# Attention products of a cross-attention + FP4 FFN kernel: operands as fp16 halves with one power of two per batch, and a new instruction order in the loop body

## What is computed

```python
# x, ctx: (32, 256, 512) f32
def xattn(q, k, v):                       # q = layernorm(x), k = v = ctx
    t, p, g = Wt @ v, Wp @ q, Wg @ k      # per batch, Wt/Wp/Wg: 256 x 256
    att = einsum('bgcd,bgcd->bg', p, g) * 0.125      # 8 groups of 32 channels
    y = Wz_g @ (att * t)                  # per group, 32 x 32
    return groupnorm(y) * gamma + beta + v
x = x + xattn(layernorm(x), ctx, ctx)
def ffn(x):                               # D = 512, H = 1408
    gate, up = q4(x) @ q4(w_gate).T, q4(x) @ q4(w_up).T
    return q4(silu(gate) * up) @ q4(w_down).T        # q4: blockwise FP4 rounding, 16 values a block
x = x + ffn(layernorm(x))
```

## Time and profile before

| | |
|---|---|
| median of 3 runs | 1738.39 us (1738.07 to 1740.09) |
| the profiled execution, own time | 1737.87 us |
| its span | 1736.0 us |
| PE busy | 1680.2 us (97%) |
| DVE busy | 1506.6 us (87%) |
| ACT busy | 825.9 us (48%) |
| POOL busy | 722.1 us (42%) |
| granted PE clock | 0.998 |

### The profile page before, as it was taken

The page is one execution under the profiler, slowest core; times in us unless marked ns, Lnnn a source line. Parts: engine busy times, 40 slices in busy tenths (PEclk is TensorE's granted clock), DMA queues, the critical chain, the costliest instruction groups (busy, mean ns, idle before and its releaser), DMA issues.

```text
span 1736.0 us, 27880 instructions
## 1 busy us (share of the span) xinstructions
PE 1680.2 (97%) x8723; PEld 919.5 (53%) x8723; DVE 1506.6 (87%) x2577; ACT 825.9 (48%) x1472; POOL 722.1 (42%) x951
## 2 busy tenths in 40 slices
PE   2799999999999999999999999999999999999999
PEld 1665555555555555555555555555555555555544
DVE  7877888889888888988898898889888988888887
ACT  3665454544445444444545444454444444545322
...
DMA packets 412150, 155.86 MB, mean 90 GB/s; under 512 B 383200, under 2 KB 384480, under 8 KB 412128
## 3 DMA queue, kind: packets, MB, share of 16 engines
...
...
## 4 chain that ended last, share of the span: by engine, by line
PE 91%; POOL 6%; DVE 1%; DMA 1%; issue 1%; ACT 0%; SPq 0%; POOLq 0%; DVEq 0%; ACTq 0%
PE pairs L550 52%; PE work L561 25%; PE work L500 5%; PE work L512 3%; PE work L527 2%; PE ubank L527 2%; POOL raw L1863 2%; POOL raw L1852 1%; POOL w_parts L1863 1%; POOL w_parts L1852 1%; DMA raw<-in_L_ffn_w_gate 0%; DMA hT_parts<-raw 0%; POOL xc L1786 0%; PE pairs L580 0%; POOL q_parts L1802 0%
## 5 line engine op out<-in xcount | busy, mean ns | idle before, releaser
L550 PE MATMUL pairs<-w_gate_hi,xT_parts 128*128 128x512 f16 (+1 forms) x1536 | 555.4, 362 | 1.5 <-DMA xT_parts<-raw 1.5
L550 PE MATMUL pairs<-w_up_hi,xT_parts 128*128 128x512 f16 (+1 forms) x1536 | 554.7, 361 | 0.0
L561 PE MATMUL work<-w_parts,hT_parts 128*128 128x512 f16 x2079 | 458.9, 379 | 0.9 <-DMA hT_parts<-raw 0.9
L561 PEld LDWEIGHTS work<-w_parts,hT_parts 128*128 128x128 f16 x2079 | 203.6, 99 | 236.0 <-issue 1.1
L550 PE MATMUL pairs<-w_up_lo,xT_parts 128*128 128x512 f16 (+1 forms) x768 | 277.5, 361 | 0.0
L550 PE MATMUL pairs<-w_gate_lo,xT_parts 128*128 128x512 f16 (+1 forms) x768 | 277.4, 361 | 0.0
L550 PEld LDWEIGHTS pairs<-w_gate_hi,xT_parts 128*128 128x128 f16 x1536 | 152.7, 99 | 162.9 <-issue 14.6
L550 PEld LDWEIGHTS pairs<-w_up_hi,xT_parts 128*128 128x128 f16 x1536 | 150.3, 98 | 146.5
L964 ACT ACTIVATE early<-pairs,w_unit 128x512 f32<-128x512 f32 (+1 forms) x192 | 124.9, 650 | 163.5 <-PE pairs L550 163.4
L873 ACT CAST raw<-hq 128x704 f16<-128x704 f32 x126 | 98.1, 779 | 180.0 <-DVE hq L1201 179.3
L1409 DVE SCALAR_TENSOR_TENSOR h<-pairs,w_unit,early 128x512 f32<-128x512 f32 (+1 forms) x192 | 135.0, 703 | 39.9 <-ACT early L964 34.7
...
## 6 DMA issues: line engine op xcount, KB each, us to landing
out<-raw SPq DMA_DIRECT2D x64, 256.0 KB, 2.1
...
```

The source lines that it names most:

```text
L550: mm = pe.matmul(pairs[:, pair, n, 0:b - a], xT[s][part][:, k, :], w1[n][wpart][:, k, a:b], start=(k == 0 and part == 0 and wpart == 0), s ...
L561: mm = pe.matmul(obank[:, :], hT[part][:, k, :], w2[wpart][:, k, :], start=(k == 0 and part == 0 and wpart == 0), stop=(k == KH - 1 and pa ...
```

## The change

It turns the operands of `mixed` and `u_rows` into fp16 halves. The context gets one power of two per batch instead of one per row: `save_rows` writes the 256 sums of squares to DRAM, `spread_rows` reads them back to every partition, `ctx_peak` takes their maximum, and `ctx_root`/`ctx_power` go on from that. The halves made for `gram` then serve `u_rows` too (`c_parts`), so `ctx_hi`, `ctx_fit_lo` and `c_wide` go; `ctx_fit` makes the hi half and an f32 copy (`c_scaled`). The Gram matrix is copied out with a fixed factor in one instruction (`gram_copy`), and DVE makes its lo half (`gram_lo`). The merged weights and Wg are split in the prologue with a power of two each (`attention_peak`, a round trip through DRAM on SP, `attention_parts`). `scale_of_u` makes the factor that undoes the scales. The orders of all bodies are rewritten.

```diff
 def mixed(b):                                        # PE
-    pe.wait_ge(gram_copied, HT * b + HT)
+    pe.wait_ge(gram_lo_done, b + 1)
...
-            mm = pe.matmul(dst[...], wgT[:, k, s * P:(s + 1) * P], gram_sb[:, k, :], ...)
+            for wpart, part in PARTS:
+                mm = pe.matmul(dst[...], wgT[wpart][:, k, s * P:(s + 1) * P], gram_sb[part][:, k, :], ...)
 def u_rows(b, s):                                    # PE
-    pe.wait_ge(c_ready, HT * b + HT)
+    pe.wait_ge(c_fit_ready, HT * b + HT)
...
-            mm = pe.matmul(u_bank(b, s), wuT[wpart][...], c_wide[part][:, k, :], ...)      # fp32r
+            mm = pe.matmul(u_bank(b, s), wuT[wpart][...], c_parts[:, k, part, :], ...)     # fp16
 def gram_copy(b):                                    # ACT
-    for s in range(HT):
-        activation(gram_sb[:, s, :], gram_bank(b)[:, s * C:(s + 1) * C], Identity, scale=c_norm[:, 3, s:s + 1])
+    activation(gram_sb[0], gram_bank(b)[:, 0:HT * C], Identity, scale=SS)
+def save_rows(b):                                    # ACT
+    act.wait_ge(c_squared, HT * b + HT)
+    at_least(act, c_rows_spread, 16 * b)
+    nc.scalar.dma_start(c_rows, c_norm[:, 0, :]).then_inc(c_rows_saved, 16)
+def spread_rows(b):                                  # ACT
+    act.wait_ge(c_rows_saved, 16 * b + 16)
+    at_least(act, c_peaked, b)
+    nc.scalar.dma_start(c_all[:], c_rows ... .to_broadcast([P, HT * P])).then_inc(c_rows_spread, 16)
 def ctx_fit(b):                                      # ACT
     for s in range(HT):
         activation(c_parts[:, s, 0, :], c_in[:, s, :], Identity, scale=c_norm[:, 2, 0:1])
+        activation(c_scaled[:, s, :], c_in[:, s, :], Identity, scale=c_norm[:, 2, 0:1])
-def ctx_hi(b): ...                                   # ACT, two activations
-def ctx_fit_lo(b): ...                               # ACT, two activations
+def ctx_peak(b):                                     # DVE
+    dve.wait_ge(c_rows_spread, 16 * b + 16)
+    tensor_reduce(c_norm[:, 1, 1:2], c_all[:, :], AX_X, ALU.max).then_inc(c_peaked, 1)
+def scale_of_u(b):                                   # DVE
+    tensor_scalar(u_scale[:, :], wu_pow[:, 5, :], c_norm[:, 3, 0:1], None, ALU.mult)
+def gram_lo(b):                                      # DVE
+    dve.wait_ge(gram_copied, b + 1)
+    scalar_tensor_tensor(out=gram_sb[1], in0=gram_bank(b)[:, 0:HT * C], scalar=SS, in1=gram_sb[0], mult, subtract)
 def ctx_root(b):                                     # POOL
-    pool.wait_ge(c_squared, HT * b + HT)
+    pool.wait_ge(c_peaked, b + 1)
 # PE body
+    u_rows(i + 1, 0)
     gram(i + 1)
     hidden(j, 0, 0)
     mixed(i + 1)
-    u_rows(i + 1, 0)
     u_rows(i + 1, 1)
 # DVE body, from variance(i + 1) to gated(j + 1, 1, 0)
     variance(i + 1)
-    ln1_means(i + 2)
+    x_lo(j + 1)
+    ln1_moments(i + 2, 0)
     gated(j, 0, 2)
     h_first(j)
+    ctx_power(i + 2)
     h_scales(j, 0)
-    h_units(j, 0)
+    residual(j + 2, 0)
     h_y(j)
-    residual(j + 2, 0)
-    emit(j - 1, 1, 16 * (i - 1))
     x1_moments(j + 2)
-    h_snap_add(j)
+    h_units(j, 0)
+    emit(j - 1, 1, 16 * (i - 1))
     x1_mean(j + 2)
+    ln1_moments(i + 2, 1)
+    h_snap_add(j)
+    ln1_means(i + 2)
     h_snap_back(j)
     h_quant(j, 0)
     h_quant(j, 1)
     h_lo(j, 0)
+    normalise2(j + 2)
     h_lo(j, 1)
-    normalise2(j + 2)
     gated(j + 1, 1, 0)
 # DVE prologue
-    attention_lo()
+    attention_peak()
...
+    ctx_peak(0)
     weight_round(0)
     ctx_power(0)
+    attention_parts()
+    scale_of_u(0)
```

More of the change, by code:

```diff
@@ L466, in body @@
                 turn_x(j + 1, 1)
+                turn_h(j)
+                store(j - 1, 1)
                 if ahead:
                     turn_c(i + 2)
-                store(j - 1, 1)
-                turn_h(j)
-                if ahead:
                     turn_q(i + 2)
@@ L1508, in _ @@
             weight_scales(1, 1)
+            gram_lo(0)
             sum_pg(0, 0)
@@ L1514, in _ @@
             copy_group(0)
+            ctx_peak(1)
             ctx_power(1)
@@ L1517, in _ @@
             variance(0)
+            scale_of_u(1)
             ln1_moments(1, 1)
@@ L1563, in _ @@
             h_y(0)
+            gram_lo(1)
             weight_round(10)
@@ L1586, in _ @@
             h_lo(0, 0)
+            ctx_peak(2)
             ctx_power(2)
+            scale_of_u(2)
             x_scales(2)
@@ L1610, in body @@
                 normalise2(j + 1)
+                if more:
+                    gram_lo(i + 1)
+                x_first(j + 1)
                 h_snap_add(j - 1)
@@ L1613, in body @@
                 h_quant(j - 1, 0)
-                x_first(j + 1)
+                h_lo(j - 1, 0)
                 h_quant(j - 1, 1)
+                x_scales(j + 1)
+                x_y(j + 1)
                 if more:
                     sum_pg(i + 1, 0)
-                h_lo(j - 1, 0)
-                x_scales(j + 1)
-                x_y(j + 1)
-                if ahead:
-                    ln1_moments(i + 2, 0)
-                    ctx_power(i + 2)
+                h_lo(j - 1, 1)
                 gated(j, 0, 0)
@@ L1626, in body @@
                     sum_pg(i + 1, 1)
[L1627 removed]
+                    copy_group(i + 1)
                 x_add(j + 1)
                 x_back(j + 1)
[L1630 to L1633 removed]
                 gated(j, 0, 1)
                 if ahead:
[L1636 removed]
+                    ctx_peak(i + 2)
+                x_quant(j + 1)
                 if more:
                     variance(i + 1)
+                x_lo(j + 1)
+                if ahead:
+                    ln1_moments(i + 2, 0)
+                gated(j, 0, 2)
+                h_first(j)
+                if ahead:
+                    ctx_power(i + 2)
+                h_scales(j, 0)
+                if more:
+                    residual(j + 2, 0)
+                h_y(j)
+                if more:
+                    x1_moments(j + 2)
+                h_units(j, 0)
+                emit(j - 1, 1, 16 * (i - 1))
+                if more:
+                    x1_mean(j + 2)
+                if ahead:
+                    ln1_moments(i + 2, 1)
+                h_snap_add(j)
                 if ahead:
                     ln1_means(i + 2)
[L1641 to L1653 removed]
                 h_snap_back(j)
@@ L1657, in body @@
                 h_lo(j, 0)
-                h_lo(j, 1)
                 if more:
                     normalise2(j + 2)
+                h_lo(j, 1)
                 gated(j + 1, 1, 0)
+                if ahead:
+                    scale_of_u(i + 2)
                 if more:
+                    x_first(j + 2)
                     residual(j + 3, 1)
+                    x_scales(j + 2)
+                    x_y(j + 2)
                 if ahead:
@@ L1926, in body @@
                 j = HT * i
+                columns(i + 1)
                 if ahead:
                     ctx_root(i + 2)
-                columns(i + 1)
-                if ahead:
-                    ctx_lo(i + 2, 0)
                 columns_affine(i + 1)
-                if ahead:
-                    ctx_lo(i + 2, 1)
-                    add_ctx(i + 2, 0)
-                    ln1(i + 2)
                 root2(j + 2)
                 if ahead:
+                    ln1(i + 2)
+                    ctx_lo(i + 2, 0)
+                    add_ctx(i + 2, 0)
                     add_ctx(i + 2, 1)
+                    ctx_lo(i + 2, 1)
                     q_lo(i + 2, 0)
```

248 lines of the change are left out of this document (140 added, 108 removed).

## The result

| | before | after |
|---|---|---|
| median of all runs, us | 1738.32 | 1846.74 |
| lowest and highest, us | 1738.06 to 1740.09 | 1843.97 to 1851.26 |
| ratio, 95% interval | | 1.0624, 1.0611 to 1.0638 |
| span of the profiled execution, us | 1736.0 | 1844.9 |
| loop's first PE instruction, us | 168.37 | 197.32 |

The kernel is slower by 6.2%, some 108 us. The forecast was 1770 us with a range of 1745 to 1800, so its sign is right and its size is not. The 108 us split into 197.32 - 168.37 = 28.95 us ahead of the loop, where 7.5 were forecast, and 29 x (53.11 - 50.33) = 80.6 us in the loop (53.11 is the mean of its bodies), where 25 were; the last body and the end take about 1 us less than before.

What follows compares the result with a forecast made beforehand. PE was taken as the bound, with 0.52 us of room before a wait. From 1737.9 us, +25 for 29 bodies at +0.85, -0.6 for the last body and +7.5 for the prologue gave 1770 us, range 1745 to 1800.

Steps and rivals of the forecast that it cites:

- The bound and the place: Loop: PE is the bound, and its nearest wait, for the transposed h ahead of output(j), is 0.52 us away.
- The matmuls, -0.6 us a body: PE in the loop: mixed and u_rows in fp16 take 3.91 us in place of 4.54, 0.6 us less per body.
- The new operations on DVE at nothing: DVE in the loop: gram_lo, ctx_peak and scale_of_u, 1.2 us a body, fit idle time and cost nothing.
- The stretch at 17.0 us: DVE from variance to the second h_lo(j): 15.41 us becomes 17.0, so PE waits 1.1 us ahead of output(j).
- A wait on POOL: DVE's h_snap_add finds root2's pow running on POOL: 0.35 us a body, bounds 0 and 0.56.
- Rival 2: POOL and DVE collide more than once; one 1.27 us collision inside the stretch gives 1807 us, half gives 1788; chance 0.22.
- The 1.48 us row: Old trace: a normalise2 issued 0.07 us behind a POOL addition took 1.48 us, cited as agreeing with the blocking rule.
- The transpose at 5.2 us: Loop: the transpose of h that output(j) needs lands 5.2 us after SP issues it.
- The prologue at +7.5 us: Ahead of the loop: 5 us at ctx_root(0) plus 2.5 at ctx_root(1) make +7.5 us, bounds +3 and +15.
- I take 5: Prologue: the DRAM round trip and a maximum make POOL's ctx_root(0) 5 us late, between 3 and 13.
- `attention_parts` at nothing: Prologue: attention_parts adds some 4 us on DVE, where weight_round(1) had about that much lead, so costs nothing.
- The range: Whole kernel: 1745 to 1800 us, down to rival 3's near-cancelling and up into Rival 2, without its worse half.

Runs made afterwards that it cites:

- e2_before_moved: The kernel before with only DVE's order from variance to the last h_lo as changed, and POOL's root2 ahead of ln1: 1759.41 us.
- e13_gram_lo: The kernel of e12_start2 with gram_lo moved between h_snap_add and h_snap_back in DVE's body: 1729.75 us, ratio 0.9943.
- e3_pool_short: The changed kernel with POOL's add_ctx, ctx_lo and q_lo of batches 3 and on cut to 32 of 512 columns, for measuring only: 1776.05 us.
- e7_stretch_short: The kernel of e1_stretch with POOL's passes cut to 32 columns as in e3_pool_short: 1787.75 us.
- e1_stretch: The changed kernel with DVE's order between variance and the last h_lo put back as before: 1845.41 us.
- e6_fit_later: The kernel of e4_old_orders with ctx_fit in one piece behind the third silu and affine, and gated(j + 1, 1, 0) ahead of normalise2: 1777.42 us.
- e4_old_orders: The changed kernel with the loop body's order on all five engines as before, as far as its parts exist; prologue as changed: 1794.68 us.
- e9_fit_early: The kernel of e6_fit_later with ctx_peak, ctx_power and ctx_fit earlier and POOL reordered so ctx_lo runs beside h_first: 1754.42 us.
- e5_prologue: The changed kernel with only the part ahead of the loop reordered on DVE, ACT and POOL: 1832.06 us.
- e12_start2: The kernel of e9_fit_early with the prologue order of e5_prologue and further places ahead of the loop reordered on PE, ACT, DVE: 1734.78 us.

## Why the prediction was right or wrong

- **The bound and the place.** Right: PE was the bound, the nearest wait was the one for the transposed h, and DVE's stretch from `variance` on is what pushed it over. e2_before_moved has that wait by itself, 0.64 us a time.
- **The matmuls, -0.6 us a body.** Right. In e13_gram_lo `mixed` and `u_rows` take 1.31 + 2.59 = 3.90 us, and it gets the whole difference, 50.33 - 49.67 = 0.66. In the changed kernel PE's waits swallow it.
- **The new operations on DVE at nothing.** Right for the loop, given a place: e13_gram_lo runs them all at PE's pace. The cover of `gram_lo` is thin, though: one place later costs 0.25 us a body.
- **The stretch at 17.0 us.** Nearly right: without meetings it takes 16.64 us, in e2_before_moved and in e3_pool_short alike, 0.4 less than its terms add up to. By the prediction's own sum that makes a wait of 0.7 us in place of 1.1, and e2_before_moved has 0.64. When the meetings are cut, 50.67 - 49.67 = 1.0 us a body is left of the loss. That this is close to 1.1 is luck: PE's waits in e3_pool_short are only 0.5 us a body, and the number covers all orders of the changed kernel; e7_stretch_short shows that it isn't this stretch's alone.
- **"A wait on POOL", 0.35 us.** This is the step that failed in the loop. The meeting it named cost nothing: `root2`'s pow ran from 972.88 to 973.43, `h_snap_add` was issued into it at 973.03 and took 1.60 us, and over the steady stretch it takes 1.61 us beside such a short operation and 1.62 without. And the step allowed for one short meeting where the long passes `ctx_lo`, `add_ctx` and `q_lo` lengthen five of DVE's passes in every body: one each of `h_lo`, `x_lo`, `x_y`, `normalise1` and `normalise2`. e3_pool_short prices them at 53.11 - 50.67 = 2.44 us a body, 71 us of the 108. Rival 2 was this mechanism; it had the two meetings inside the stretch in the right place, but its price, one meeting of 1.27 us, was half of what came, and its 1807 us lay outside the range. It counted four long passes and left out the two `q_lo`. It looked for collisions in the stretch only and trusted that DVE had 5.9 us of room elsewhere; 4.2 us of longer passes took most of that, and the waits came back in other places when the stretch was shortened (e1_stretch).
- **The rule that rival 2 cites.** The Trainium skill, "SBUF — State Buffer", section "Who interferes with whom", says that a VectorE pass with two SBUF inputs contends with a GpSimd instruction that reads SBUF, that one with a single input does so only in its two-port modes, that reductions stay out, and that the one issued first holds the other up for its whole length. For GpSimd's passes of 512 columns the rows agree: `h_lo`, `x_lo` and `x_y` in the changed kernel and `h_y` in e6_fit_later are 0.7 to 1.1 us longer when they begin second, `h_lo` keeps its length when it begins first, `gated`, with one of its inputs in PSUM, keeps its 0.74 us, and `h_first`, a reduction, was not lengthened by a `ctx_lo`. `normalise1` and `normalise2` (each a `tensor_scalar`) are 0.84 longer; no row tells in which mode they ran. The 1.48 us row that the prediction sets beside the rule is a `normalise2` too, not a `tensor_tensor`. For the short operations the rows don't agree: `h_snap_add` has two SBUF inputs and began behind the pow, and took no longer.
- **The transpose at 5.2 us.** Held for `turn_h(j)`. For `turn_h(j-1)` it took 6.2 in the mean, with the new round trip and the later load of x in flight, and PE waited 0.46 us a body there. It is 5.2 again in e4_old_orders, e6_fit_later, e9_fit_early and e13_gram_lo, which keep the round trip and load x at the head of ACT's body. That speaks for the load of x, but no run moved it alone, so the cause is argued, not shown.
- **The prologue at +7.5 us, bounds 3 and 15.** Wrong, 29. The first term, "I take 5", was mis-sized: the round trip put `ctx_root(0)` 9.6 us late. The second, `attention_parts` at nothing behind a lead of `weight_round(1)`, failed: DVE had no lead left after it had waited 6.5 us for the same round trip, and all 8.3 us stand in the chain that ended last. With both behind it, `ctx_root(1)` ran at 77.31, 19.5 us late, where 2.5 more had been forecast. e5_prologue gets 14.1 us of the 29 back by order alone, e12_start2 19.6; the last 9 go with the new work or were not found.
- **The range** failed since two of its bounds did, the prologue's 15 us and rival 2's single meeting, both in the same direction.
